# A decoder layer on one core: the attention's values weighed by f16 high and low parts instead of f32

## What is computed

```python
q = (x @ Wq).reshape(N, S, HEADS, HEAD_DIM).transpose(0, 2, 1, 3)
k = (x @ Wk).reshape(N, S, HEADS, HEAD_DIM).transpose(0, 2, 1, 3)
v = (x @ Wv).reshape(N, S, HEADS, HEAD_DIM).transpose(0, 2, 1, 3)
logits = jnp.einsum('nhid,nhjd->nhij', q, k) * scale
logits = logits + causal[None, None, :, :]
attn = jax.nn.softmax(logits, axis=-1)
out = jnp.einsum('nhij,nhjd->nhid', attn, v)
return out.transpose(0, 2, 1, 3).reshape(N, S, HEADS * HEAD_DIM) @ Wo + bo
```

## Time and profile before

| | |
|---|---|
| median of 3 runs | 890.45 us (888.92 to 891.08) |
| profiled execution | 890.64 us, span of the trace 889.4 us |
| attention's steps | about 17 to 355 us of the span |
| granted clock of PE, mean | 0.996 of 2.4 GHz |
| weighing of the values, L741 | 768 records, 50.3 us busy |

### The profile page before, as it was taken

How to read it: one execution, slowest core, us unless ns; L and a number is a source line. 1 busy time by engine, 2 the same in 40 slices (tenths; PEclk the granted TensorE clock), 3 DMA queues, 4 the chain that set the end, 5 groups by cost and what they waited for, 6 DMA issues and landing times. The chain is left out here.

```text
span 889.4 us, 23089 instructions
## 1 busy us (share of the span) xinstructions
PE 859.9 (97%) x8094; PEld 680.0 (76%) x8094; DVE 606.1 (68%) x1669; ACT 557.2 (63%) x1251; POOL 377.8 (42%) x492
## 2 busy tenths in 40 slices
PE   5999999999999999999999999999999999999996
PEld 3888788888888888767676666676788888887864
DVE  3667588776667675756666667869677767766655
ACT  4988776777676776655756565564455555555555
POOL 1634354343433475324444332544534444444433
PEclk9999999999999999999999999999999999999999
DMA  9733424342424331410000000399423323333226
GB/s 317 207 126 113 142 97 152 119 160 96 143 94 138 103 119 49 62 42 2 1 1 1 2 1 1 105 393 356 158 52 50 49 44 50 49 50 50 43 27 195
DMA packets 61579, 88.04 MB, mean 99 GB/s; under 512 B 17279, under 2 KB 46527, under 8 KB 61343
## 3 DMA queue, kind: packets, MB, share of 16 engines
q1 hardware_dynamic: 53439, 75.52, 25.8%
q0 software_dynamic: 7488, 10.27, 7.3%
q10 hardware_dynamic: 544, 0.79, 0.3%
HBM read 56.00 MB, written 30.56 MB: 97 GB/s over the span
## 5 line engine op out<-in xcount | busy, mean ns | idle before, releaser
L648 POOL TENSOR_SCALAR prob<-prob,rden 128x128 f32<-128x128 f32 (+1 forms) x256 | 122.9, 498 | 183.1 <-DVE rden L949 183.0
L2219 PE MATMUL ps<-slots,e 128*128 128x128 f16 x1872 | 190.0, 219 | 2.2 <-DVE xs L2386 2.1
L2219 PEld LDWEIGHTS ps<-slots,e 128*128 x1872 | 152.6, 97 | 35.3 <-issue 4.4
L843 ACT ACTIVATE prob<-prob,nmx 128x128 f32<-128x128 f32 (+1 forms) x256 | 113.2, 444 | 29.8 <-DVE nmx L943 29.8
L2227 PE MATMUL ps<-e,xT 128*128 x312 | 117.3, 378 | 0.0
L2316 ACT ACTIVATE slots<-slots 128x512 f32<-128x512 f32 x78 | 49.1, 630 | 106.8 <-DVE slots L2370 106.8
L943 DVE CUSTOM_DVE_ANT_0 prob<-ps,mask 128x128 f32<-128x128 f32 (+1 forms) x256 | 73.7, 353 | 41.5 <-PE ps L730 41.5
L31 PE MATMUL ps<-xT,wqkv 128*128 128x256 f16 x768 | 97.2, 278 | 2.0 <-ACT slots L850 1.4
L31 PEld LDWEIGHTS ps<-xT,wqkv 128*128 128x128 f16 x768 | 73.4, 99 | 18.3 <-issue 6.9
L1731 POOL DMA_INDIRECT xg<-rows_x,dst x39 | 40.9, 1049 | 106.3 <-DVE mask L2359 103.0
L2228 PE MATMUL ps<-e,xT 128*128 x312 | 85.0, 273 | 0.0
(11 more groups left out here) (267 smaller groups left out, 1855.3 us busy)
## 6 DMA issues: line engine op xcount, KB each, us to landing
halves<-parted SPq DMA_DIRECT2D x36, 512.0 KB, 2.9
piece<-in_L_ffn_ew SPq DMA_DIRECT2D x32, 512.0 KB, 4.5
e<-halves SPq DMA_DIRECT2D x16, 1024.0 KB, 15.2
piece<-in_L_ffn_sh_w SPq DMA_DIRECT2D x4, 512.0 KB, 8.8
sw<-halves SPq DMA_DIRECT2D x4, 512.0 KB, 6.8
rows_x<-xs SPq DMA_DIRECT2D x4, 512.0 KB, 7.4
xs<-back_y SPq DMA_DIRECT2D x8, 256.0 KB, 4.4
out<-xs SPq DMA_DIRECT2D x8, 256.0 KB, 2.1
```

The lines of the kernel that those rows point to most:

```text
L648: PO.tensor_scalar(prob[u][:, h, r], prob[u][:, h, r], rden[u][:, h, t:t + 1], 1.0, ALU.mult, ALU.mult).then_inc(normed, 1)
L843: SC.activation(at, at, ACT.Exp, bias=nmx[u][:, h, t:t + 1], scale=-1.0, accum_out=den[u][:, h, t:t + 1]).then_inc(exped, 1)
L2219: yield PE.matmul(ps[:, 2 * u + q, (k % 4) * P:(k % 4) * P + P], w[ch][h], xgT[u][j][:, ch, :], start=n == 0, stop=n == 3 * DC - 1)
```

## The change

The turned probabilities and the values are written as f16 high and low parts, and the weighing becomes three f16 products for each f32 one. ACT writes the high parts (of both pairs of the probabilities, one instruction for each, and of the values), DVE the low parts (two subtractions for the probabilities, one for the values). pT is now two buffers (high, low), and so are the values. POOL's normalisation multiplies by 4096 as well, the values are scaled by 8, and heads_high and heads_low divide by the product. In DVE's loop values_low(j) comes first, ahead of masks(j+1), and probs_low(j) comes behind reciprocals(j+1, 1), where the copy stood ahead of them. scores waits for each pair's pT_lo apart; weigh_values waits for v_lo.

```diff
@@ attention_tensor
                 def scores(m):
-                    if m >= 2:
-                        PE.wait_ge(pT_out, 2 * (m - 1))
                     for p in range(2):
+                        if m >= 2:
+                            PE.wait_ge(pT_lo, 2 * (m - 2) + p + 1)
                         PE.wait_ge(qk_out, 2 * m + p + 1)
...
                 def weigh_values(m):
-                    PE.wait_ge(pT_out, 2 * (m + 1))
-                    PE.wait_ge(v_out, min(m + 2, STAGES))
+                    PE.wait_ge(v_lo, min(m + 2, STAGES))
                     for p in range(2):
+                        PE.wait_ge(pT_lo, 2 * m + p + 1)
                         for t, key, at in ((0, 0, 0), (1, 0, P), (1, 1, 2 * P)):
...
+                            for n, (i, j) in enumerate(HILO):
+                                for h in range(2):
+                                    r = slice(HD * h, HD * h + HD)
+                                    mm = PE.matmul(ps[r, 1, (2 * p + t) * P:(2 * p + t) * P + P],
+                                                   v_parts[m % 2][i][:, key, p, r], pT[j][:, 2 * p + h, at:at + P],
+                                                   start=key == 0 and n == 0, stop=key == t and n == len(HILO) - 1,
+                                                   skip_group_check=True)
@@ attention_scalar
-                def probs_turned(m):
-
-                    SC.wait_ge(p_turned, 2 * m + 2)
+                def probs_high(m, p):
+                    SC.wait_ge(p_turned, 2 * m + p + 1)
                     if m >= 1:
                         SC.wait_ge(o_mm, m)
-                    SC.copy(pT[:, 2:4, :], ps[:, 4:6, 0:384]).then_inc(pT_out, 1)
-
-                def values_out(m):
+                    h = 2 * p
+                    SC.copy(pT[0][:, h:h + 2, :], ps[:, 2 + h:4 + h, 0:384]).then_inc(pT_hi, 1)
+
+                def values_high(m):
...
@@ attention_vector
+                def values_low(m):
+                    VE.wait_ge(v_hi, m + 1)
+                    VE.scalar_tensor_tensor(v_parts[m % 2][1][:, :, :, :],
+                                            ps[:, 1, :].rearrange("p (t m n) -> p t m n", t=2, m=2), V_UP / WS,
+                                            v_parts[m % 2][0][:, :, :, :], ALU.mult, ALU.subtract).then_inc(v_lo, 1)
+
+                def probs_low(m, p):
+                    VE.wait_ge(pT_hi, 2 * m + p + 1)
+                    h = 2 * p
+                    VE.tensor_tensor(pT[1][:, h:h + 2, :], ps[:, 2 + h:4 + h, 0:384], pT[0][:, h:h + 2, :],
+                                     ALU.subtract).then_inc(pT_lo, 1)
...
                 for j in range(FIRST, LAST + 1):
+                    if 0 <= j < STAGES:
+                        values_low(j)
                     if 0 <= j + 1 < STAGES:
                         masks(j + 1, 0)
                         masks(j + 1, 1)
...
                     if 0 <= j - 1 < STAGES:
                         heads_low(j - 1)
-                    if 0 <= j < STAGES:
-                        probs_turned(j)
                     if 0 <= j + 1 < STAGES:
                         reciprocals(j + 1, 1)
+                    if 0 <= j < STAGES:
+                        probs_low(j, 0)
+                        probs_low(j, 1)
```

## The result

The changed kernel takes 931.08 us (median of 4 runs, 928.3 to 933.69), the kernel before 890.77 in the same set; the ratio is 1.0471 (95% interval 1.0447 to 1.0495). It is slower by 4.7%; 924 us had been forecast, in a range of 908 to 945.

The account below looks back on a forecast made before the run. TensorE, busy 97% of the span, was taken to bound the kernel. The terms 19.5+4.2-1.2+7.1+0.6+3.1 summed to +33.3 us against 890.6, so 924 us, 3.7% slower, range 908 to 945.

Parts of the forecast that it names:

- PE's block: TensorE's weighing in each stage: 36 f16 matmuls take 1.0 us instead of 1.3, 0.31 us less per stage.
- C: Weighing on TensorE: the column halves do not overlap in f16, so the block takes 2.0 us; 929 us, chance 0.06.
- D: Weighing on TensorE: loads are not hidden either, 0.081 us per pair, 2.9 us per stage; about 942 us, chance 0.03.
- The round: VectorE from one stage's first mask to the next: 8.34 us plus the rest of its stage work, probs_low waiting for ScalarE.
- the sixteen in which DVE's round was forecast as the longest: Stages 1, 3, 5, 11-13, 15-17, 21, 23-25, 28-30, set by VectorE's mask-to-mask time: +19.5 us together.
- the four of ACT: Stages 2, 4, 6 and 7, where ScalarE's mask-to-mask time is longest: +4.2 us together.
- the four of PE: Stages 19, 20, 26 and 27, where TensorE has a long share and stays longest: -1.2 us together.
- the four turned ones: Stages 10, 14, 18 and 22, where TensorE turns inputs and waits for the now later prep_vector: +7.1 us together.
- The last step: End of the attention, first mask to vw_tensor: 15.6 us instead of 12.2, +3.4 (+3.1 after the shorter last weighing).
- Rival B: TensorE's clock falls after idle of some 2 us: nine stages, 1.3 us each where it counts, +12, 936 us; chance 0.11.
- Rival A: Only load counts, not order; VectorE and ScalarE keep up and TensorE's gain stands: 882 us, faster; chance 0.05.
- The signs: Expected in the trace: TensorE idle before most weighings; masks behind values_low, on average no earlier than 1.4 us into stages.

Follow-up runs that it names:

- the run with both fillings: Changed kernel with two late piece_low shares ahead of the second reciprocals, prep_vector ahead of probs_low, first piece_high right behind values_high: 898.51 us, ratio 1.0122.
- the first filling run: Changed kernel with up to four late piece_low shares per iteration moved from behind probs_low into VectorE's two idle spells: 915.36 us, ratio 1.0321.
- the filled versions: Changed kernel with ready work moved into idle spells of VectorE (915.36 and 905.6 us), then also of ScalarE (898.51 us).

## Why the prediction was right, step by step

- **PE's block.** Forecast 1.0 us of matmuls, measured 1.20 us for 36 records with the last one's length in it (148.07), a pace of (1.20-0.22)/35 = 0.028: two halves side by side. Against 1.53 before that is 0.33 us less, 0.31 forecast. Rivals C and D are out. The Trainium skill's 81 ns per load-and-matmul pair ("TensorE: Matmul & The Clock Gate", Back-to-back issue gap) is three times what this trace has; its "TensorEngine Tiling (Array Packing)", PSUM Bottleneck, warns that once tiling has made TensorE faster, the copies out of PSUM may become the bottleneck. This trace agrees in part: the copies and subtractions out of PSUM set the time, but through what waits for what, with DVE busy 70% and ACT 62% of the span.
- **The operations.** probs_low 0.95 (0.97 forecast), values_low 0.69, ACT's copy 0.79, two of them in 1.48 us: right.
- **The round.** M+7.77 for the end of probs_low in stage 12, forecast 7.81. M to M over the stages, after less before: the sixteen in which DVE's round was forecast as the longest +18.8 (forecast 19.5 and 0.6 of onset), the four of ACT +5.0 (4.2), the four of PE -0.7 (-1.2), the four turned ones, where inputs are turned, +8.5 (7.1; the terms as written, three times 12.4 and 13.1, give 6.9), 8 and 9 -0.4 (0).
- **The last step.** First mask to vw_tensor takes 18.3 us (368.74 to 387.01) against 12.2: +6.1, not +3.4. This term was mis-sized, for the most part by the clock. PE, last steps, and under them the same steps of the run with both fillings, where the granted clock stayed at 1.00:

```profile
378.89 2.13 PE L744 MATMUL ps<-pT,v 128*64 128x128 f16 x36 [3.56 <-DVE v L959]
...
381.86 2.61 PE L702 MATMUL ps<-ident,prob 128*128 128x128 f32 x12
...
387.01 1.16 PE L31 MATMUL ps<-wst 128*120 128x384 f16 x6 [1.23 <-DVE wst L326]
```

```profile
352.84 1.20 PE L744 MATMUL ps<-pT,v 128*64 128x128 f16 x36 [3.02 <-DVE v L961]
...
354.46 1.47 PE L702 MATMUL ps<-ident,prob 128*128 128x128 f32 x12
...
358.68 2.13 PE L31 MATMUL ps<-wst 128*120 128x384 f16 x12 [1.44 <-DVE wst L326]
```

After 3.56 us of idle PE the weighing takes 2.13 instead of 1.20 and the transposes 2.61 instead of 1.47. From that weighing to vw_tensor are 8.12 us, at the full clock 5.84: 2.3 of the 2.7 us by which the term was short.

- **Rival B, the clock,** came true in part. It had nine stages and +12 us; the clock was granted at 1.2 GHz for a few us six times in the attention, once before, and where its price can be read it is 0.3 us in each of three stages and the 2.3 of the last step. In stage 14 (first mask to first mask, columns as above) the mean was 0.87:

```profile
172.42:185.85 13.43, 11.76 (x120) 10.11 (x120) 9.30 (x31) 9.65 (x25) 3.69 (x9) 0.87 0.21 75
232.63:243.65 11.02, 11.02 (x124) 9.56 (x120) 8.34 (x31) 8.18 (x23) 3.40 (x8) 1.00 0.21 74
```

Stages 10, 14 and 18 each have such a fall and each took 0.3 us more than forecast (12.73, 13.43, 12.74 against 12.4, 13.1, 12.4). Stage 22, with no fall, took its 12.42; in the first filling run, which leaves prep_vector where it was, 10 and 18 had no fall and took 12.39 and 12.42. The second row is stage 19: PE without a gap, 0.34 below before, as forecast.
- **Rival A** (order does not matter) is out by the filling run: 15.7 us with the same work.
- **The signs.** The first mask starts 2.5 us into stages 1 to 30 on average (1.1 before; the limit set was 1.4). Of the four stages that were to show no idle PE ahead of L744, 19, 20 and 27 show none, and 26 shows 1.56 us. "Stage 12 about 13 us" was wrong: 11.48. Its rest R had been read as 4.43 us and came out 1.3 shorter, as the four shares of piece_low in it take 1.42 us and not 2.79. In the kernel before one of them, beside POOL's L655, took 1.49 us and the one ahead of it, beside L648 and L655, 0.70; the 77 that met no work of POOL took 0.42 on average. DVE and POOL before, then DVE after:

```profile
143.22 2.79 DVE L592 SCALAR_TENSOR_TENSOR parted<-piece,parted 128x256 f16<-128x256 f32 x4
143.97 1.43 POOL L655 TENSOR_TENSOR xs<-xs,bo 128x512 f32<-128x512 f32 x1
```

```profile
156.95 1.42 DVE L594 SCALAR_TENSOR_TENSOR parted<-piece,parted 128x256 f16<-128x256 f32 x4
```

- **What was left.** The profiled span is 37.3 us longer, 33.3 had been forecast. Of the 4.0 between, the turned stages make 1.4 and the last step 2.7; what comes behind it took 1.6 more instead of 0.3 less, with one more fall of the clock 5 us after the experts' first matmul (that this fall is the cause was not tested); stage 0 and what lies ahead of it gave back 1.5, which is luck (the first mask starts at 15.9 to 18.4 us in the profiled executions of all kernels), and the other terms cancel nearly. The other 3 us to 931 are the scatter of the executions: the profiled one took 928.3.

## What to carry to other kernels

Before work is moved from a full engine to two half-empty ones, follow one round through their queues: an operation that waits for the other engine costs its wait plus everything queued behind it, whatever the busy shares say. Price it from one mask to the next, not from the sum of durations. If such a split is wanted, fill the idle spells ahead of the new waits with work that is ready; here that gave back 33 of 40 us (from 4.7% to 1.2% over the kernel before), and it was not enough. Placing the values earlier without that only moved the waits: at the new place, too, something waited with ready work queued behind it.

## What was not expected of the hardware

- The order of the other engines' queues moved TensorE's clock: the changed kernel's six falls in the attention became two, one or none in the filled versions, where PE's idle spells are shorter. Idle of 0.8 us in stage 11 of the kernel after left the clock at 1.00, and during the 3.56 us above it fell to the 1.2 GHz level. But the length of one spell does not decide: 1.75 us in the kernel before were followed by a fall, the 3.02 us in the filled version were not. Stage 11 of the kernel after, columns as above:

```profile
137.17:147.94 10.77, 9.97 (x120) 8.52 (x116) 8.72 (x33) 7.99 (x23) 3.40 (x8) 1.00 0.17 68
```

- f16 loads of 64 columns with matmuls of 128 columns, two column halves in turn, kept a pace of 28 ns per pair, half of the 56 ns of the unpaired ones.
- VectorE's piece_low took 0.42 us where no GpSimd work ran beside it (77 times before, 132 after). Where one started while GpSimd's addition (L655 before, L657 after) was running, it ended 0.28 us after the addition did: 1.49 us twice before, 1.12 and 1.48 after, and five of 1.15 to 1.43 in the run with both fillings. So a duration read off the trace of before can depend on what ran beside it there.
